# In-degrees of the first three node chunks from VectorE sums and one matmul each, reciprocal degrees through memory

## The reference, cut to what matters

```python
deg = segment_sum(ones_like(edge_dst), edge_dst, num_segments=N)
deg_inv = 1.0 / maximum(deg, 1.0)
# _sage_layer, called twice with the same deg_inv
msg = h[edge_src]
agg = segment_sum(msg, edge_dst, num_segments=h.shape[0])
mean = agg * deg_inv[:, None]
return h @ W_self + mean @ W_neigh + b
```

## Time and profile before

| | before |
|---|---|
| median of 3 runs | 855.65 us (853.54 to 860.68) |
| profiled execution: its own time | 855.76 us |
| span of the profile | 854.1 us |
| TensorE busy | 833.4 us, 98% of the span |
| VectorE busy | 461.1 us, 54% |
| ScalarE busy | 177.8 us, 21% |
| GpSimd busy | 455.0 us, 53% |
| mean granted TensorE clock | 0.994 of full |
| chain that ended last | PE 88%, DVE 4%, DMA 3% |

### The profile page before, as it was taken

The page is one execution under the profiler, slowest core; times in us unless marked ns, Lnnn a source line. Parts: engine busy times, 40 slices in busy tenths (PEclk is TensorE's granted clock), DMA queues, the critical chain, the costliest instruction groups (busy, mean ns, idle before and its releaser), DMA issues.

```text
span 854.1 us, 10997 instructions
## 1 busy us (share of the span) xinstructions
PE 833.4 (98%) x4295; PEld 710.1 (83%) x4295; DVE 461.1 (54%) x714; ACT 177.8 (21%) x218; POOL 455.0 (53%) x343
## 2 busy tenths in 40 slices
PE   7999999999999999999999999999999999999996
PEld 5888888888898899788888888778889889988885
DVE  5556568200016565897645578675655535455555
ACT  4211132010211112553223212212222122200000
POOL 4118886887888767887788788778620000000000
PEclk9999999999999999999999999999999999999999
DMA  9977966362776444569776669258877748555551
GB/s 300 374 313 257 356 186 194 105 192 64 223 223 189 114 84 116 199 249 317 279 266 247 234 222 297 53 148 239 224 242 264 230 143 286 201 197 197 197 191 44
DMA packets 99482, 180.56 MB, mean 211 GB/s; under 512 B 15474, under 2 KB 75898, under 8 KB 94048
## 3 DMA queue, kind: packets, MB, share of 16 engines
q1 hardware_dynamic: 60144, 124.17, 44.0%
q10 hardware_dynamic: 26896, 40.65, 13.4%
q0 software_dynamic: 12384, 14.95, 7.7%
HBM read 107.08 MB, written 72.43 MB: 210 GB/s over the span
## 4 chain that ended last, share of the span: by engine, by line
PE 88%; DVE 4%; DMA 3%; ACT 2%; issue 2%; SPq 1%; ACTq 1%; DVEq 0%
PE ps L1408 23%; PE ps L1524 19%; PE ps L1436 12%; PE ps L1558 10%; PE ps L1467 10%; PE ps L1541 9%; DMA first_rows<-in_L_gnn_W_neigh 2%; PE ps L1392 1%; DMA spare<-in_x 1%; ACT outb L743 1%; PE ps L1347 1%; PE ps L1357 1%; PE ps L1456 1%; SPq L417 0%; ACTq L733 0%
## 5 line engine op out<-in xcount | busy, mean ns | idle before, releaser
L641 POOL DMA_INDIRECT adj_out<-loops,idx_out x160 | 242.3, 1514 | 70.1 <-issue 62.3
L641 POOL DMA_INDIRECT adj_in<-mult,idx_in x160 | 197.0, 1231 | 89.9 <-issue 89.9
L1524 PE MATMUL ps<-u 128*128 128x512 f32 x840 | 190.7, 389 | 1.5 <-DVE u L1063 1.5
L1524 PEld LDWEIGHTS ps<-u 128*128 128x128 f32 x840 | 157.6, 188 | 34.4 <-issue 1.6
L1408 PE MATMUL ps<-wx 128*128 128x512 f32 x480 | 113.3, 393 | 3.4 <-ACT wx L700 2.7
L1436 PE MATMUL ps<-wx 128*128 128x512 f32 (+1 forms) x576 | 109.4, 351 | 1.6 <-ACT outb L743 1.6
L1408 PEld LDWEIGHTS ps<-wx 128*128 128x128 f32 x480 | 88.9, 188 | 23.3 <-ACT wx L700 4.3
L1436 PEld LDWEIGHTS ps<-wx 128*128 128x128 f32 x576 | 93.9, 189 | 17.2 <-ACT outb L743 2.2
L1408 PE MATMUL ps<-u 128*128 128x512 f32 x432 | 98.2, 389 | 0.0
L1541 PE MATMUL ps<-u,panel_tiles 128*128 128x512 f32 (+1 forms) x400 | 95.5, 398 | 1.9 <-DVE s L1130 1.9
L1467 PE MATMUL ps<-wx,u 128*128 128x256 f32 (+5 forms) x640 | 96.0, 312 | 0.0
(11 more groups left out here) (168 smaller groups left out, 734.6 us busy)
## 6 DMA issues: line engine op xcount, KB each, us to landing
left_scr<-u SPq DMA_DIRECT2D x7, 2560.0 KB, 9.6
u<-left_scr SPq DMA_DIRECT2D x7, 2560.0 KB, 9.7
xt_scr<-wx ACTq DMA_DIRECT2D x10, 1024.0 KB, 10.1
u<-xt_scr SPq DMA_DIRECT2D x10, 1024.0 KB, 5.0
wx<-xt_scr SPq DMA_DIRECT2D x16, 512.0 KB, 3.8
adj_in<-u POOLq DMA_DIRECT2D x4, 1600.0 KB, 25.6
adj_out<-u POOLq DMA_DIRECT2D x4, 1600.0 KB, 15.4
wx<-adj_in SPq DMA_DIRECT2D x5, 1280.0 KB, 8.1
```

Source lines behind the costliest of these rows:

```text
L641: pool.indirect_dma_start(table, bass.IndirectOffsetOnAxis(ap=index[0:EP, j:j + 1], axis=0), counts[0:EP, j:j + 1], None, bounds_check=CEL ...
L1524: ins = nc.tensor.matmul(ps[:, product_bank(g, i, p), :], left_op[n % 2][:, p, k, left, :], right_op[n % 2][:, k, right, :], start=(not on ...
```

## The change

The change does three things in `mean0`, and some bookkeeping.

1. For chunks 0, 1 and 2 VectorE first adds the ten source blocks of a panel: a `tensor_reduce` with the block index k as the innermost axis, read in steps of 1 KB (256 floats in a panel of a pair; 2560 values read for 256 results, or 5120 for 512), into `sacc`, and then a copy to float32r, `colsum`. TensorE makes the sum over partitions with a single matmul of ones, placed after the first feature block of chunks 0 and 2 and after the second of chunk 1 (`d == c % 2`). Chunk 3 keeps its ten matmuls ahead of its blocks.
2. The matmuls with one row of weights and VectorE's copies to `dinv` are gone. SP stores each chunk's reciprocal row to memory behind the fetch of block d = 6, and loads the whole as a column, element by element, once, after the loop.
3. The bias load (512 KB) moves from behind m = 0 to behind that load; `bias` and `colsum` share one place.

Some semaphores are merged (`pool_set`, `ones_ready` counts to 4), with the same instructions around them.

```diff
@@ sync @@
                 if m in (15, 23):
                     load_chunk_1(2 + m // 17)
+                if d == 6:
+                    t0, n = CHUNKS[c]
+                    sp.wait_ge(dinv_row_done, c + 1)
+                    sp.dma_start(dinv_scr[lines(CHUNKS[c])].rearrange("(a j) -> a j", a=1), dinv_row[0:1, c % 2, 0:n * T]
+                                 ).then_inc(dinv_stored[c % 2], 16)
                 if m == 0:
                     load_block(0, 0, 0)
-                    sp.dma_start(bias[:, :], b1.rearrange("(a d) -> a d", a=1).broadcast_to([P, D])).then_inc(bias_full, 16)
...
             load_block(0, 1, 0)
+            for s in range(2):
+                sp.wait_ge(dinv_stored[s], 16 * 2)
+            sp.dma_start(dinv[:, :], dinv_scr.rearrange("(t p) -> p t", p=P), allow_slow_non_contiguous=True).then_inc(dinv_in, 16)
+            sp.wait_ge(deg_full, 4)
+            sp.dma_start(bias[:, :], b1.rearrange("(a d) -> a d", a=1).broadcast_to([P, D])).then_inc(bias_full, 16)
             sp.wait_ge(h_sum, KD * 4)
             load_block(0, 1, 1)
@@ vector @@
                 if d == 0:
+                    if c < 3:
+                        dve.wait_ge(m1_full[c], 16 * n // 2)
+                        nc.vector.tensor_reduce(sacc[:, 0:width].rearrange("p (n j) -> p n j", n=n // 2),
+                                                m1_panels[c][:, :, :, :].bitcast(F32).rearrange("p k n j -> p n j k"), AX_X, ALU.add
+                                                ).then_inc(colsum_done, 1)
+                        dve.wait_ge(colsum_done, 2 * c + 1)
+                        nc.vector.tensor_copy(colsum[:, 0:width], sacc[:, 0:width]).then_inc(colsum_done, 1)
                     dve.wait_ge(deg_full, c + 1)
                     if c >= 2:
-                        dve.wait_ge(dcol_full, c - 1)
+                        dve.wait_ge(dinv_stored[c % 2], 16)
...
-                if d == 5:
-                    dve.wait_ge(dcol_full, c + 1)
-                    nc.vector.tensor_copy(dinv[:, t0:t0 + n], ps[:, 6 + c % 2, 0:n]).then_inc(dcol_read, 1)
@@ tensor @@
+            def degrees(c, width, exact):
+                if c < 2:
+                    pe.wait_ge(s0_free, s0_bank_free(6 + c))
+                else:
+                    pe.wait_ge(deg_read, c - 1)
+                pe.wait_ge(colsum_done, 2 * c + 2)
+                bank = ps[:, 6 + c % 2, 0:width]
+                if exact:
+                    ins = nc.tensor.matmul(bank, ones_r[:, :].bitcast(F32), sacc[:, 0:width], start=True, stop=True)
+                else:
+                    ins = nc.tensor.matmul(bank, ones_r[:, :], colsum[:, 0:width], start=True, stop=True)
+                ins.then_inc(deg_full, 1)
+
             def mean0(exact):
...
-                    for k in range(NT):
-                        ins = nc.tensor.matmul(ps[:, 6 + c % 2, 0:width].rearrange("p (n j) -> p n j", n=n // 2), typed(ones_r[0:rows(k), :], exact),
-                                               typed(panels[0:rows(k), k, :, :], exact), start=(k == 0), stop=(k == NT - 1))
-                    ins.then_inc(deg_full, 1)
+                    if c == 3:
+                        pe.wait_ge(deg_read, c - 1)
+                        for k in range(NT):
+                            ins = nc.tensor.matmul(ps[:, 6 + c % 2, 0:width].rearrange("p (n j) -> p n j", n=n // 2),
+                                                   typed(ones_r[0:rows(k), :], exact), typed(panels[0:rows(k), k, :, :], exact),
+                                                   start=(k == 0), stop=(k == NT - 1))
+                        ins.then_inc(deg_full, 1)
...
-                        if d == 2:
-                            pe.wait_ge(dinv_row_done, c + 1)
-                            for i in range(n):
-                                ins = nc.tensor.matmul(ps[:, 6 + c % 2, i:i + 1], dinv_row[0:1, c % 2, i * T:(i + 1) * T],
-                                                       ones_nt[0:1, 0:1], start=True, stop=True)
-                            ins.then_inc(dcol_full, 1)
+                        if c < 3 and d == c % 2:
+                            degrees(c, width, exact)
```

More of the change, by code:

```diff
@@ L85, in build @@
         keys_scr = dram("keys_scr", [E])
+        dinv_scr = dram("dinv_scr", [PER])
         edges_scr = dram("edges_scr", [2, PAD_E], I32)
@@ L90, in build @@
         base = -(-nc.sbuf_base // 32) * 32
-        U_AT, WX_AT, R_AT, E_AT, END = (base + n for n in (0, 81920, 163840, 188416, 197120))
+        U_AT, WX_AT, R_AT, E_AT, B_AT, END = (base + n for n in (0, 81920, 163840, 188416, 197120, 201216))
         sb("arena", [P, (END - base) // 4], F32)
@@ L115, in build @@
         ones_r = sb("ones_r", [P, P], F32R)
-        bias = sb("bias", [P, D], F32)
+        bias = at("bias", [P, D], F32, B_AT)
+        colsum = at("colsum", [P, WIDE], F32R, B_AT)
         ident = sb("ident", [P, P], F32)
@@ L242, in build @@
         edges_in = sem("edges_in")
-        pads_set = sem("pads_set")
-        zeros_ready = sem("zeros_ready")
-        ident_zero = sem("ident_zero")
+        pool_set = sem("pool_set")
         ident_ready = sem("ident_ready")
@@ L315, in build @@
         s0_free = sem("s0_free")
+        colsum_done = sem("colsum_done")
         deg_full = sem("deg_full")
@@ L318, in build @@
         dinv_row_done = sem("dinv_row_done")
-        dcol_full = sem("dcol_full")
-        dcol_read = sem("dcol_read")
-        dsum_zero = sem("dsum_zero")
+        dinv_stored = sems("dinv_stored", 2)
+        dinv_in = sem("dinv_in")
         dsum_part = sem("dsum_part")
@@ L610, in _ @@
         def _(pool):
-            nc.gpsimd.memset(pad_ids, NO_NODE).then_inc(pads_set, 1)
-            nc.gpsimd.memset(ident[:, :], 0.0).then_inc(ident_zero, 1)
-            pool.wait_ge(ident_zero, 1)
+            nc.gpsimd.memset(pad_ids, NO_NODE).then_inc(pool_set, 1)
+            nc.gpsimd.memset(ident[:, :], 0.0).then_inc(pool_set, 1)
+            pool.wait_ge(pool_set, 2)
             nc.gpsimd.affine_select(out=ident[:, :], in_=ident[:, :], compare_op=ALU.not_equal, fill=1.0, base=0,
@@ L619, in _ @@
                                ).then_inc(edges_copied, 16)
-            pool.wait_ge(pads_set, 1)
+            pool.wait_ge(pool_set, 2)
             ends = bass.AP(tensor=edges_scr.tensor, offset=0, ap=[[4 * PAD_E, 1], [PAD_E, 2], [WINDOW + E, 2], [1, WINDOW]])
             pool.dma_start(ends, pad_ids.rearrange("p (i e c) -> p i e c", i=2, e=2)).then_inc(edges_pad, 16)
-            nc.gpsimd.memset(zeros, 0.0).then_inc(zeros_ready, 1)
+            nc.gpsimd.memset(zeros, 0.0).then_inc(pool_set, 1)
             pool.wait_ge(edges_copied, 32)
@@ L634, in clear @@
                     pool.dma_start(runs[a, :, :], zeros).then_inc(done, 16)
-            pool.wait_ge(zeros_ready, 1)
+            pool.wait_ge(pool_set, 3)
             pool.wait_ge(w_hi_done, KD)
@@ L643, in put @@
                     bounds_check=CELLS - 1, oob_is_err=False).then_inc(done, 16)
-            pool.wait_ge(ones_ready, 3)
+            pool.wait_ge(ones_ready, 4)
             pool.wait_ge(flag_ready, 1)
@@ L1019, in _ @@
             nc.vector.memset(ones_r[:, :].bitcast(F32), 1.0).then_inc(ones_ready, 1)
-            nc.vector.memset(dsum[:, :], 0.0).then_inc(dsum_zero, 1)
+            nc.vector.memset(dsum[:, :], 0.0).then_inc(ones_ready, 1)
             nc.vector.memset(pairs[:, :], 0.0).then_inc(keys_used, 1)
@@ L1030, in _ @@
             dve.wait_ge(keys_used, 1)
-            dve.wait_ge(dsum_zero, 1)
+            dve.wait_ge(ones_ready, 4)
             for t in range(NT):
@@ L1242, in _ @@
                 u1_low(1, t0)
+            dve.wait_ge(dinv_in, 16)
             for t in range(NT):
@@ L1450, in mean0 @@
                     pe.wait_ge(m1_full[c], 16 * n // 2)
-                    if c < 2:
-                        pe.wait_ge(s0_free, s0_bank_free(6 + c))
-                    else:
-                        pe.wait_ge(dcol_read, c - 1)
-                    for k in range(NT):
-                        ins = nc.tensor.matmul(ps[:, 6 + c % 2, 0:width].rearrange("p (n j) -> p n j", n=n // 2), typed(ones_r[0:rows(k), :], exact),
-                                               typed(panels[0:rows(k), k, :, :], exact), start=(k == 0), stop=(k == NT - 1))
-                    ins.then_inc(deg_full, 1)
+                    if c == 3:
[5 more added lines that the diff above has]
+                        ins.then_inc(deg_full, 1)
                     for d in range(KD):
@@ L1488, in product_bank_free @@
                     pe.wait_ge(h_free, 32)
-                    pe.wait_ge(dcol_read, 4)
+                    pe.wait_ge(deg_read, 4)
                 elif i == 2 and p < 3:
@@ L1587, in keep_busy @@
                                      ones_r[:, :].unsqueeze(1).broadcast_to([P, BANK // P, P]), start=True, stop=True)
-            pe.wait_ge(ones_ready, 3)
+            pe.wait_ge(ones_ready, 4)
             keep_busy(9)
```

## The result

The changed kernel takes 861.97 us (median of 20 runs, 859.42 to 866.80), before 855.7 (20 runs beside it, 853.03 to 861.29). The ratio is 1.007, 95% interval 1.0055 to 1.0086: slower by 0.7%, clear of noise. Forecast was 853.9 us, and within 1%; the time lies in the range, but the change moved it the other way.

A forecast was written before the change was run, and what follows sets the result against it. TensorE, busy nearly the whole span, was taken to bound the kernel: -6.8 (work) + 1.0 + 2.25 (waits) + 1.6 (clock) = -1.9 us, from 855.76 to 853.9 us, range 852 to 866.

The forecast's parts named there:

- the price of the sum: VectorE's new reductions: 2.8 us for 2560 values and 5.5 for 5120, if the step costs nothing.
- f: Stepped sum's price as a multiple of the measured rate; waits are 3.25 + 8(f - 1), balancing the 6.8 at 1.1 to 1.2.
- the first rival: VectorE's stepped read runs at half rate, sums 5.5 and 10.8 us, +7.6, 863.4 us; chance 0.37.
- The two pages: Trainium skill: SBUF page penalises a new 16-byte line each access; DVE Perf Modes page says plain mode works for odd strides.
- TensorE's work, -6.8: Ones and narrow matmuls going, 7.25 us, less 0.47 for three single matmuls: net 6.8 us less work.
- Chunk 0, no wait: Sum and copy done by 245.5, before TensorE asks at about 246: no wait.
- Waits in chunks 1 and 2, 1.0 and 2.25: TensorE's waits for VectorE's sum and copy: 1.0 us in chunk 1, 2.25 in chunk 2.
- The clock, 1.6 once: Half clock for some 3 us after chunk 2's wait, costing 1.6 us; chunk 1's wait not counted.
- Bias load and self part: Without the bias load ahead in the queue, chunk 1's self part of m = 1 lands 1.25 us earlier, addition near 259.5.
- SP's queue: Four small stores enter; the one at m = 22 holds up chunk 3's panels, which land at 323.0; no loss counted.
- The cap: Chunk 3's panels landing at 323.0 limit the gain ahead of chunk 3 to 3.4 us; the sum stays below.
- Every stretch to be as long as before: Behind 347 us, after the stage of the change, no stretch changes its length.

The follow-up runs named there:

- e1: Changed kernel with the three new sums read in steps of one value instead of 256 (degrees not the reference's); 859.71 us, ratio 1.004 to before.
- e9: Changed kernel with 16 matmuls of no use ahead of TensorE's wait for VectorE in chunks 1 and 2; 858.11 us, ratio 1.004 to before.
- e7: Kernel before with only parts 2 and 3 of the change, plus GpSimd's diagonal writes amid the first table's scatters; 853.13 us, ratio 0.998.
- e6: Kernel before with GpSimd's two diagonal writes to the second table issued amid the first table's scatters; 857.10 us, ratio 1.0016.
- e10: Kernel before without the last 16 of the 160 indirect DMAs into the second table; 853.93 us, ratio 0.9974.
- e11: Kernel before with only parts 2 and 3 of the change, without the last 16 indirect DMAs into the second table; 852.26 us, ratio 0.9951 to before.
- e14: Changed kernel with sums as five whole-row additions, single matmul one block later in chunks 1 and 2, early diagonal writes; 854.49 us, ratio 0.998 to before.
- e15: Changed kernel keeping only chunk 0's sum on VectorE, ten matmuls of ones in chunks 1 to 3, early diagonal writes; 856.12 us, ratio 0.9994 to before.
- e12: Changed kernel with sums in steps of one value, without the last 16 indirect DMAs into the second table; 853.76 us, ratio 0.997 to before.
- e2: Changed kernel plus trial reductions at steps of 1 to 256 values, an addition and a copy in VectorE's idle time; run once for its trace.

## Why the prediction was wrong, step by step

- **The step that failed** is the price of the sum: "I take the lower value, since the only measured reductions lie on it." Those rows all read side by side, and said nothing of a step. 2560 values cost 4.6 to 4.8 us in place of 2.8, 5120 cost 9.2 in place of 5.5. With f = 1.7 the prediction's own line, 3.25 + 8(f - 1) + 3.2 - 6.8, gives +5.2 us, 861.0; 861.97 was measured. It had also worked out a balance at f of 1.1 to 1.2 (its line gives 1.24 with the clock's loss counted once and 1.04 with it twice), so that nearly the whole outcome hung on that one choice, and still gave the first rival only 0.37. The two pages were put side by side as if of one weight, where only one of them has a rule on steps.
- **TensorE's work, -6.8.** Right in size: in the changed kernel 105.3 - 6.8 + 4.51 + 4.32 and 3.5 to 4.0 for the clock give 110.8 to 111.3, measured 110.7. In e1 105.3 - 6.8 + 1.07 + 2.50 + 1.5 for the clock gives 103.6; less the 1.6 of the half clock that did not fall on the start of its stage, and with an idle gap of 0.7 at 248.3 that nothing in the trace ends, it is 102.7, measured 102.8. But see below for what it is worth.
- **Chunk 0, no wait.** Right: the sum was done at 239.4, and TensorE asked at 247.2.
- **Waits in chunks 1 and 2, 1.0 and 2.25.** Right for the price assumed (1.07 and 2.50 in e1), mis-sized with it: 4.51 and 4.32. The copy was put too low as well: 0.69 and 0.57 us, where 0.48 and 0.34 were to be the most.
- **The clock, 1.6 once.** Right in kind. The longer waits brought it down twice, for 1.5 to 1.9 and 2.0 to 2.1 us, and e9's stage gets 3 of them back.
- **Bias load and self part.** The number came out, 259.35 against the 259.5 named, but in part by luck: 0.80 us of the 1.36 are the earlier load of chunk 1's panels. Where that load left at 243.16, in e7, the addition starts at 261.18 with no bias load ahead. From the one to the other it is 18.2 to 19.9 us in the three kernels with the bias load in between (before, e6, e10) and 15.6 to 18.2 in the others that were timed, some 0.9 less by the medians, so the term of 1.25 is about right in size.
- **SP's queue.** The store at m = 22 held chunk 3's panels until 317.89 in the changed kernel, which was harmless, as TensorE was late too. The cap was right, and in the right place: in e11, e14 and e15 TensorE waits for these panels, by 1.4 to 2.7 us, until 321.95 to 324.09 (forecast 323.0).
- **"Every stretch to be as long as before" behind 347 us.** Right for the changed kernel, 506.5 us in both, but only because its late product stage left the scatters time, and wrong for the kernel that the prediction described. Had the sum cost what I took, the scatters into the second table could have taken the 1.9 us back, and more: e1 is at 859.7. I had looked at TensorE's share of the chain and not at how close the next chain ran: the last scatter started at 625.86, and the load that needs it left at 631.70. With the scatters out of the way e12 takes 853.76 us, almost the 853.9 forecast, but that is 0.2 under before with the same scatters left out, and not 1.9.

## What to carry to other kernels

Look at the step of an operand's innermost axis before costing it by a row of the same operation: on VectorE, with 4-byte values, a step of 16 bytes or more cost a reduction 1.7 to 1.8 times as much here, and one of 1 KB an addition 1.8 and a copy 1.9 times. Where a forecast has a balance point and the one unmeasured price stands near it, measure that price first, as e2 does in idle time. And before a saving on the bounding engine is counted, look for the next chain that ends at a later wait: a saving ahead of it is worth no more than that chain's slack, here some 2.3 us in the one execution profiled.

## What the runs showed of the hardware

- VectorE's price for a step, for a reduction of 2560 values, has no slope (e2, one execution): 2.82 us at 4 and 8 bytes, 4.72 at 16, 4.80 at 1 KB (5.19 at 32 bytes is the dearest).
- One wait of over 4 us cost TensorE 6: behind each of the two it ran some 3 us at half clock (granted clock 0.50), and 16 matmuls of no use in each wait brought 3 us of the stage back.
- An indirect DMA took GpSimd 1.19 us as a rule and 2 to 3.8 us beside VectorE's long additions (read from the traces, not tried). The same 160 of them took 302.0 to 311.7 us in these traces, and no run shows why.
